# Graph attention on one core: the value products of two heads placed behind the slot's job products instead of ahead of them

## The chip, the cores and the metric

The kernel runs on one core of one Trainium2 chip. The metric is the device time of the program in microseconds (us), the median of several runs. The engines meant by the short names in the rows are TensorE (PE, its weight loads PEld), VectorE (DVE), ScalarE (ACT), GpSimd (POOL) and SyncE (SP, which here only issues DMAs). Each engine works through its own instructions in order, and the engines meet only through semaphores.

## The reference

For each of B = 32 graphs with N = 256 nodes of D = 512 features, a layer norm with ReLU is followed by attention with 16 heads of 32 features, whose scores get twice the adjacency matrix added, and by an output projection and a residual:

```python
h = jnp.maximum(_layernorm(x, axis=-1), 0.0)
q = split_heads(h @ Wq.T); k = split_heads(h @ Wk.T); v = split_heads(h @ Wv.T)
a = jnp.einsum('bhnd,bhmd->bhnm', q, k) * scale + (adj + adj)[:, None]
row_nonzero = jnp.any(a != 0, axis=-1, keepdims=True)
p = softmax(where(row_nonzero, a, -inf)); p = jnp.where(jnp.isnan(p), 0.0, p)
o = jnp.einsum('bhnm,bhmd->bhnd', p, v)
out = x + merge_heads(o) @ Wo.T
```

## The kernel before, in words

One batch is one graph. A batch is cut into 16 slots, one for each head hh (L537 to L551 on TensorE, L733 on ScalarE, L967 on VectorE, L1158 on GpSimd). All engines walk through the same slots, each in its own written order; nothing is planned at run time.

**TensorE in slot hh** does, in this order:

- T: four transposes of the head's softmax numerators into the PSUM tile `pT_ps` (`transpose_probs`, L455). They wait for the exponentials of head hh and for VectorE's reading of the tile two heads back.
- S: two score products for head hh + 3 into one of three banks `s_ps` (`scores`, L439).
- V, in even slots only: the value products of heads hh-2 and hh-1, 16 short matmuls into `o_ps` (`values`, L469). They wait for the low parts of both heads' transposed probabilities (`pT_split`).
- J: the slot's share of the large products, the "jobs" of the table `JOBS` (L25): projections q and k of the next batch or of the same one (`qk`), value projections (`v`), transposes of the attention output of a batch (`o`) and the output projection (`y`). A job with 24 or 12 products is cut over slots.

The jobs use two PSUM banks in turn. At a job's first product `begin` (L360) waits until the job that used the bank before has been read out (`taken`). Three such handovers matter here:

- slot 2: the last ten products of job v2, then the first three of v3, whose bank qk3 filled until slot 1; it is free after VectorE's two operations L862 and L864.
- slot 4: y0 of the batch before; its bank was filled by v3 until late in slot 3 and is free after VectorE's L870. Slot 3 is nine products of v3 and then the four transposes of o1, whose bank v2 filled until slot 2.
- slot 14: v0 of the next batch; its bank was filled by y1 until slot 13 and is free after ScalarE's L662. Slot 15 holds v1, whose bank is not one of these.

**ScalarE in slot hh**: if hh is odd, first `copy_outputs` (L664), which copies `o_ps` out to `o_raw` and so waits for the semaphore `pv_done` of V in slot hh-1; then the exponentials of head hh+1 (L681, two instructions); then the first half of taking every job that ended in slot hh-1 (`take`, L633: L646/L648 for qk, L655 for v, L659 for o, L662 for y); then `high_probs` (L686, L692), which rounds the transposed probabilities of head hh and waits for T. The order is

```python
if hh % 2:                      # L735 to L740
    copy_outputs(b, hh // 2 - 1, first and hh < 10)
exponentials(b, hh + 1, ...)    # L745
take(kind, n, b + d, ...)       # L751
high_probs(b, hh, ...)          # L757
```

In slot 4 the taking of v3 stands ahead of the exponentials (L743), in slot 10 `split_tokens` (L702) stands at the end, and in slot 13 `copy_adj` (L710) waits for the shift of head 15.

**VectorE in slot hh**: the shifted scores of head hh+2 and their row bounds (`shift`, L901), once in four slots `any_nonzero` (L922, L932), then the second half of taking jobs, then `low_probs` (L910), which waits for `high_probs` and makes `pT_split`; in slots 3, 6, 11 and 0 statistics (L782) or `low_tokens` (L880) of a later batch follow.

**GpSimd** folds the shifted scores, divides the outputs and adds the residual. **SyncE** issues all DMAs.

Of the kernel before, what the change touches and what calls it, by code (L numbers as in the profile page):

```python
# [60 lines left out]
def jobs_at(hh, first, last):  # L61

    return [j for j in JOBS[hh] if not (first and j[2] < 0) and not (last and j[2] > 0)]
# [11 lines left out]
def attention_block(nc, x, adj, wq, wk, wv, wo_t, out):  # L75
# [23 lines left out]
    with ExitStack() as ctx:  # L99
# [256 lines left out]
        def _(pe):  # L356
# [82 lines left out]
            def scores(b, hh, early=False):  # L439
                if isinstance(b, int) and b == 0 and G <= hh < HH:  # L440

                    pe.wait_ge(late_stacked[hh % G], STACKED)
                elif hh % HH < G:

                    pe.wait_ge(stacked[hh % G], stack_count(hh // HH, b))
                if not early:

                    pe.wait_ge(shifted, head_no(b, hh) + (1 - bank_before(hh)))
                stack = qk_stack[:, hh // HH, hh % G, :, hh % HH // G, :]
                for t in range(NT):  # L450
                    end = nc.tensor.matmul(s_ps[SCORE_BANK[hh]][:, t * N:(t + 1) * N], stack[:, 0, t * P:(t + 1) * P],  # L451
                                           stack[:, 1, :], start=True, stop=True)
                end.then_inc(scores_ready, 1)

            def transpose_probs(b, hh, early):  # L455

                pe.wait_ge(exp_done, head_no(b, hh) + 1)
                if not early:
                    pe.wait_ge(pT_split, head_no(b, hh) - 1)
                elif hh == 1:  # L460

                    pe.wait_ge(taken["v"], count("v", 0, 0))
                for m in range(NT):
                    for t in range(NT):
                        end = nc.tensor.transpose(pT_ps[hh % 2][:, m * N + t * P:m * N + (t + 1) * P],  # L465
                                                  probs[hh % 2][:, t, m * P:(m + 1) * P], ident[:, :])
                end.then_inc(pT_ready, 1)

            def values(b, hh, early):  # L469

                if hh % HH == 0:

                    pe.wait_ge(taken["v"], count("v", 2 * (hh // HH) + 1, b))
                if hh % 2 == 0 and not early:

                    pe.wait_ge(o_copied, b * PAIRS + hh // 2)

                pe.wait_ge(pT_split, head_no(b, hh) + 1)
                for t in range(NT):
                    q = (hh % 2) * NT + t  # L480
                    ps = o_ps[:, q * P:(q + 1) * P]
                    for m in range(NT):
                        hi = pT_hi[hh % 4][:, m, t * P:(t + 1) * P]
                        lo = pT_lo[hh % 4][:, m, t * P:(t + 1) * P]
                        v = v_parts[:, m, hh, :]
                        nc.tensor.matmul(ps[:, 0:LOW + HD], hi, v[:, 0:LOW + HD], start=m == 0, stop=False)  # L486
                        end = nc.tensor.matmul(ps[:, 0:HD + 1], lo, v[:, 0:HD + 1], start=False, stop=m == NT - 1)  # L487
                end.then_inc(pv_done, 1)
# [48 lines left out]
            def body(b, odd, first, last):  # L537
                for hh in range(HEADS):
                    transpose_probs(b, hh, first and hh < 2)
                    if hh + AHEAD < HEADS:  # L540
                        scores(b, hh + AHEAD)
                    elif not last:
                        scores(b + 1, hh + AHEAD - HEADS)

                    for was in range(hh - 2, hh) if hh % 2 == 0 else ():
                        if was >= 0:
                            values(b, was, first and was < 2)
                        elif not first:
                            values(b - 1, HEADS + was, False)
                    for kind, n, d, start, stop in jobs_at(hh, first, last):  # L550
                        job(kind, n, d, start, stop, b, odd)  # L551
                for i, (kind, n, d) in last_in.items():
                    last_in[i] = (kind, n, d - 1)

            for b in range(B):
                body(b, b % 2, b == 0, b == B - 1)
# [652 lines left out]
```

## Time and profile before

| what | value |
|---|---|
| median of 3 runs | 1252.07 us (1252.06 to 1252.55) |
| the profiled execution, its own time | 1249.15 us |
| its span, first to last instruction | 1247.4 us |
| mean granted TensorE clock | 0.997 of full speed |
| TensorE busy with matmuls | 1209.6 us (97%), 12856 of them |
| VectorE busy | 1088.7 us (87%) |
| ScalarE busy | 1029.7 us (83%) |
| GpSimd busy | 905.8 us (73%) |

The busy time of an engine is the sum of its instruction records without their overlaps. A record of TensorE is longer than the step to the next one, since matmuls overlap; what an instruction costs there is read from start to start. Records of ScalarE and VectorE too overlap the next one slightly. One batch takes 37.91 us in the middle of the run (slot 0 begins at 601.41 us, that of the next batch at 639.32).

### The profile page before, as it was taken

What the parts mean: (1) busy time and instruction counts of PE and PEld (TensorE: products, weight loads), DVE (VectorE), ACT (ScalarE), POOL (GpSimd) and SP (SyncE); (2) the same over time, 40 slices, a digit from 0 to 9 for tenths busy, and PEclk for the clock granted to TensorE, in tenths of its full rate; (3) what the DMA queues carried; (4) which work ended last, traced back from release to release, by engine and by line L of the source; (5) the groups of instructions that cost most, each with busy time, mean ns of one, the idle gap of its engine ahead of it and who ended that gap; (6) DMA issues with size and microseconds to landing.
All of it is one profiled execution on the core that took longest, in us unless ns stands there. A gap on an engine that the chain in (4) does not pass through costs nothing.

```text
span 1247.4 us, 42107 instructions
## 1 busy us (share of the span) xinstructions
PE 1209.6 (97%) x12856; PEld 1087.1 (87%) x12856; DVE 1088.7 (87%) x3500; ACT 1029.7 (83%) x2398; POOL 905.8 (73%) x1268
## 2 busy tenths in 40 slices
PE   6899999999999999999999999999999999999997
PEld 5788988888889888889888888888898888898896
DVE  7798888888888888888888888898888888888887
ACT  5788888888888888888888888888888888888886
POOL 5587777777777777777677777777777777776775
PEclk9899999999999999999999999999999999999999
DMA  6567555676656676565775565765556755556643
GB/s 227 122 143 166 140 129 142 141 174 150 146 120 146 151 169 149 134 139 138 161 169 135 121 154 135 177 154 135 127 148 149 170 144 135 137 137 169 146 106 90
DMA packets 157431, 181.73 MB, mean 146 GB/s; under 512 B 80641, under 2 KB 90369, under 8 KB 157313
## 3 DMA queue, kind: packets, MB, share of 16 engines
q1 hardware_dynamic: 157312, 179.90, 59.6%
q8 instruction: 105, 1.72, 0.6%
q14 instruction: 14, 0.11, 0.0%
HBM read 46.14 MB, written 16.78 MB: 50 GB/s over the span
## 4 chain that ended last, share of the span: by engine, by line
issue 49%; POOL 45%; POOLq 2%; DVE 2%; PE 1%; DMA 1%; ACT 0%; SPq 0%; DVEq 0%
POOL fold L1117 14%; POOL o_raw L1091 6%; POOL bounds L1123 6%; POOL y L1109 6%; POOL mask L1084 3%; POOL o L1097 3%; POOL h L1076 2%; POOL factor L1088 2%; POOL rstd L1065 2%; PE job_ps L374 1%; DMA x_in<-x 1%; POOL minus_mean L1060 1%; POOL var_eps L1062 0%; POOL wo_lo L1130 0%; POOLq L1119 0%
## 5 line engine op out<-in xcount | busy, mean ns | idle before, releaser
L1117 POOL TENSOR_TENSOR fold<-minus 128x512 f32<-128x512 f32 x256 | 327.2, 1278 | 247.5 <-DVE bounds L901 247.5
L681 ACT ACTIVATE probs<-minus,bounds 128x256 f32<-128x256 f32 x1024 | 464.6, 508 | 28.3 <-DVE bounds L901 28.2
L910 DVE TENSOR_TENSOR pT_lo<-pT_ps,pT_hi 128x512 f16<-128x512 f32 x512 | 350.0, 684 | 90.0 <-ACT pT_hi L692 85.9
L901 DVE CUSTOM_DVE_ANT_0 minus<-s_ps,adj_now 128x256 f32<-128x256 f32 x1024 | 389.3, 418 | 6.3 <-ACT probs L681 4.6
L692 ACT ACTIVATE pT_hi<-pT_ps 128x512 f16<-128x512 f32 x512 | 306.2, 598 | 86.1 <-PE pT_ps L465 84.4
L374 PE MATMUL job_ps<-hT,w_hi 128*128 128x256 f16 x2048 | 350.5, 273 | 0.4 <-DVE hT L857 0.4
L465 PE MATMUL pT_ps<-ident,probs 128*128 128x128 f32 x2048 | 308.0, 273 | 1.8 <-ACT probs L681 1.6
L374 PE MATMUL job_ps<-hT,w_lo 128*128 128x256 f16 x1024 | 279.1, 273 | 0.0
L465 PEld LDWEIGHTS pT_ps<-ident,probs 128*128 128x128 f32 x2048 | 242.0, 141 | 19.2 <-ACT probs L681 2.5
L451 PE MATMUL s_ps<-qk_stack 96*128 96x256 f32 x1024 | 247.5, 323 | 5.1 <-DMA qk_stack<-qk_parts 5.1
L1123 POOL TENSOR_TENSOR bounds<-fold 128x256 f32<-128x256 f32 x256 | 197.6, 772 | 25.1 <-POOL fold L1117 9.6
L374 PEld LDWEIGHTS job_ps<-hT,w_hi 128*128 128x128 f16 x2048 | 180.9, 98 | 24.5 <-issue 0.6
L374 PE MATMUL job_ps<-w_hi,hT 128*128 128x256 f16 x1016 | 190.1, 273 | 4.8 <-ACT y L662 4.6
L486 PE MATMUL o_ps<-v_parts,pT_hi 128*128 128x65 f16 x2048 | 156.9, 192 | 3.7 <-DVE pT_lo L910 0.9
L451 PEld LDWEIGHTS s_ps<-qk_stack 96*128 96x128 f32 x1024 | 155.0, 191 | 6.2 <-DMA qk_stack<-qk_parts 5.9
L487 PE MATMUL o_ps<-v_parts,pT_lo 128*128 128x33 f16 x2048 | 150.1, 179 | 0.0
L486 PEld LDWEIGHTS o_ps<-v_parts,pT_hi 128*128 128x128 f16 x2048 | 123.7, 97 | 18.6 <-DVE pT_lo L910 7.1
L374 PE MATMUL job_ps<-w_lo,hT 128*128 128x256 f16 x508 | 138.4, 272 | 0.0
L487 PEld LDWEIGHTS o_ps<-v_parts,pT_lo 128*128 128x128 f16 x2048 | 126.8, 96 | 0.0
L374 PEld LDWEIGHTS job_ps<-w_hi,hT 128*128 128x128 f16 x1016 | 96.9, 98 | 21.1 <-ACT y L662 7.6
L374 PE MATMUL job_ps<-wo_hi,oT_hi 128*128 128x512 f32 x256 | 107.4, 419 | 6.8 <-DVE v_parts L870 6.6
L374 PEld LDWEIGHTS job_ps<-hT,w_lo 128*128 128x128 f16 x1024 | 99.9, 98 | 11.8
(92 smaller groups left out, 1835.3 us busy)
## 6 DMA issues: line engine op xcount, KB each, us to landing
qk_stack<-qk_parts SPq DMA_DIRECT2D x756, 128.0 KB, 2.3
x_in<-x SPq DMA_DIRECT2D x32, 512.0 KB, 4.8
x_res<-x SPq DMA_DIRECT2D x32, 512.0 KB, 3.9
out<-y SPq DMA_DIRECT2D x64, 256.0 KB, 2.1
adj_in<-adj SPq DMA_DIRECT2D x32, 256.0 KB, 3.5
qk_stack<-qk_parts SPq DMA_DIRECT2D x24, 64.0 KB, 2.0
w_in<-wq SPq DMA_DIRECT2D x2, 512.0 KB, 5.6
w_in<-wk SPq DMA_DIRECT2D x2, 512.0 KB, 6.4
```

What stands on the lines that cost most here:

```text
L374: end = nc.tensor.matmul(dst, lhs[a](k), rhs[c](k), start=i == 0, stop=i == len(terms) - 1)
L451: end = nc.tensor.matmul(s_ps[SCORE_BANK[hh]][:, t * N:(t + 1) * N], stack[:, 0, t * P:(t + 1) * P], stack[:, 1, :], start=True, stop=True)
L465: end = nc.tensor.transpose(pT_ps[hh % 2][:, m * N + t * P:m * N + (t + 1) * P], probs[hh % 2][:, t, m * P:(m + 1) * P], ident[:, :])
L486: nc.tensor.matmul(ps[:, 0:LOW + HD], hi, v[:, 0:LOW + HD], start=m == 0, stop=False)
L487: end = nc.tensor.matmul(ps[:, 0:HD + 1], lo, v[:, 0:HD + 1], start=False, stop=m == NT - 1)
L681: end = nc.scalar.activation(probs[hh % 2][:, t, :], minus[hh // 2 % 2][:, hh % 2, t, :], ACT.Exp, bias=bounds[:, hh // 2 % 4, 2 * (hh % 2 ...
L692: nc.scalar.activation(pT_hi[hh % 4][:, :, :], pT_ps[hh % 2][:, :].rearrange("p (m n) -> p m n", m=NT), ACT.Copy).then_inc(pT_high, 1)
L901: end = nc.vector.tensor_tensor_reduce(out=minus[pair % 2][:, hh % 2, t, :], in0=s_ps[SCORE_BANK[hh]][:, t * N:(t + 1) * N], in1=adj_now[: ...
L910: nc.vector.tensor_tensor(pT_lo[hh % 4][:, :, :], pT_ps[hh % 2][:, :].rearrange("p (m n) -> p m n", m=NT), pT_hi[hh % 4][:, :, :], ALU.sub ...
L1091: nc.gpsimd.tensor_tensor(raw[:, :, :, 0:HD], raw[:, :, :, 0:HD], raw[:, :, :, LOW:LOW + HD], ALU.add).then_inc(o_added, 1)
L1117: nc.gpsimd.tensor_tensor(f1[:, :, :], src[:, :, 0:N // 2], src[:, :, N // 2:N], ALU.add).then_inc(folded1, 1)
L1123: nc.gpsimd.tensor_tensor(f2, f1[:, :, 0:N // 4], f1[:, :, N // 4:N // 2], ALU.add).then_inc(folded2, 1)
```

## The change

In the loop of TensorE over the slots, the value products of the last two heads are written behind the loop over the slot's jobs. No instruction is added or removed, no wait is changed, and no other engine's code is touched. Odd slots have no value products and stay as they are.

```diff
                     elif not last:
                         scores(b + 1, hh + AHEAD - HEADS)
 
+                    for kind, n, d, start, stop in jobs_at(hh, first, last):
+                        job(kind, n, d, start, stop, b, odd)
                     for was in range(hh - 2, hh) if hh % 2 == 0 else ():
                         if was >= 0:
                             values(b, was, first and was < 2)
                         elif not first:
                             values(b - 1, HEADS + was, False)
-                    for kind, n, d, start, stop in jobs_at(hh, first, last):
-                        job(kind, n, d, start, stop, b, odd)
                 for i, (kind, n, d) in last_in.items():
                     last_in[i] = (kind, n, d - 1)
```

## Rows read from the trace of the kernel before

**Rows 1.** The page, part 1: busy us, share of the span, instructions.
```profile
PE 1209.6 (97%) x12856; PEld 1087.1 (87%) x12856; DVE 1088.7 (87%) x3500; ACT 1029.7 (83%) x2398; POOL 905.8 (73%) x1268
```

**Rows 2.** Waits of PE over the whole span: us in total, times, longest us.
```profile
PE job_ps L374 <- DVE v_parts L870: 6.6, 29, 0.2
...
PE job_ps L374 <- ACT y L662: 4.6, 28, 0.2
...
PE o_ps L486 <- DVE pT_lo L910: 0.9, 2, 0.5
```

**Rows 3.** Timeline of PE, slots 2 to 5: start us, length us, operation, count, idle before.
```profile
607.21 0.38 PE L374 MATMUL job_ps<-w_hi,hT 128*128 128x256 f16 x2
...
608.63 0.60 PE L465 MATMUL pT_ps<-ident,probs 128*128 128x128 f32 x4
...
611.42 0.20 PE L486 MATMUL o_ps<-v_parts,pT_hi 128*128 128x65 f16 x1
...
611.85 0.18 PE L487 MATMUL o_ps<-v_parts,pT_lo 128*128 128x33 f16 x1
612.26 0.50 PE L374 MATMUL job_ps<-wo_hi,oT_hi 128*128 128x512 f32 x1 [0.23 <-DVE v_parts L870]
...
613.75 0.60 PE L465 MATMUL pT_ps<-ident,probs 128*128 128x128 f32 x4
```

**Rows 4.** Timeline of ACT, slots 3 and 4.
```profile
607.48 0.39 ACT L670 ACTIVATE o_raw<-o_ps 128x260 f32<-128x260 f32 x1
607.76 0.90 ACT L681 ACTIVATE probs<-minus,bounds 128x256 f32<-128x256 f32 x2
608.56 0.37 ACT L655 ACTIVATE v_parts<-job_ps 128x256 f16<-128x256 f32 x1
609.27 0.60 ACT L692 ACTIVATE pT_hi<-pT_ps 128x512 f16<-128x512 f32 x1 [0.33 <-PE pT_ps L465]
```

**Rows 5.** Timeline of DVE, slots 2 to 4.
```profile
607.24 0.42 DVE L864 SCALAR_TENSOR_TENSOR qk_parts<-job_ps,qk_parts 128x256 fp32r<-128x256 f32 x1
...
609.90 0.69 DVE L910 TENSOR_TENSOR pT_lo<-pT_ps,pT_hi 128x512 f16<-128x512 f32 x1 [0.50 <-ACT pT_hi L692]
...
611.78 0.42 DVE L870 SCALAR_TENSOR_TENSOR v_parts<-job_ps,v_parts 128x256 f16<-128x256 f32 x1
```

**Rows 6.** Timeline of ACT, slots 11 to 15.
```profile
626.99 0.40 ACT L670 ACTIVATE o_raw<-o_ps 128x260 f32<-128x260 f32 x1
...
628.05 0.61 ACT L692 ACTIVATE pT_hi<-pT_ps 128x512 f16<-128x512 f32 x1
...
635.35 0.58 ACT L662 ACTIVATE y<-job_ps 128x512 f32<-128x512 f32 x1
...
637.85 0.40 ACT L655 ACTIVATE v_parts<-job_ps 128x256 f16<-128x256 f32 x1
638.11 0.62 ACT L692 ACTIVATE pT_hi<-pT_ps 128x512 f16<-128x512 f32 x1
```

**Rows 7.** Timeline of PE, slots 11 to 15.
```profile
627.17 0.60 PE L465 MATMUL pT_ps<-ident,probs 128*128 128x128 f32 x4
...
634.64 0.48 PE L451 MATMUL s_ps<-qk_stack 96*128 96x256 f32 x2
635.99 0.28 PE L374 MATMUL job_ps<-w_hi,hT 128*128 128x256 f16 x1 [0.17 <-ACT y L662]
...
637.31 0.60 PE L465 MATMUL pT_ps<-ident,probs 128*128 128x128 f32 x4
```

**Rows 8.** One stretch of DVE, slot 15 to slot 2: stretch, its length, DVE busy, clock.
```profile
600.87:606.84 5.97, 5.66 (x20) 1.00 1.00 227
```

**Rows 9.** Timeline of weight loads and of PE, last batch, slot 14, which has no job.
```profile
1235.48 0.42 PEld L465 LDWEIGHTS pT_ps<-ident,probs 128*128 128x128 f32 x4
...
1235.51 0.64 PE L465 MATMUL pT_ps<-ident,probs 128*128 128x128 f32 x4
```

**Rows 10.** Stretches of the whole core after a 4.89 us wait: length, PE, PEld, DVE, ACT, POOL, clock.
```profile
46.00:50.00 4.00, 3.42 (x27) 2.82 (x28) 3.99 (x14) 3.13 (x8) 2.61 (x5) 0.50 0.96 216
...
600.00:637.90 37.90, 37.42 (x403) 33.72 (x401) 33.51 (x109) 31.78 (x76) 27.97 (x40) 1.00 0.64 147
```

## The prediction

> **What bounds the kernel now.** I read the page first: TensorE is busy for 97% of the span, VectorE for 87%, ScalarE for 83% [rows 1]. One batch in the middle confirms it: 37.42 of 37.90 us at full clock [rows 10]. So TensorE's own stream sets the time, and only what makes it longer or leaves a hole in it counts. The second view is the list of its waits. Two of them come back about once a batch, short ones: y0 in slot 4 waits for VectorE's L870 (29 times, 6.6 us), v0 in slot 14 for ScalarE's L662 (28 times, 4.6 us). A wait for the value products' own input exists twice, 0.9 us in all [rows 2]. This tells two things: the order of before has almost nothing left to win for the value products, and in slots 4 and 14 the job already starts at the very moment its bank comes free. The third view is the timeline of three engines over one batch, from which I take the steps below. I write T, S, V, J for the parts of a slot, as in the section on the kernel.
>
> **What moves.** Per even slot V (16 matmuls) costs 0.46 us from first start to the next possible one (611.42 to 611.85 plus one step of 0.03) [rows 3]. J now begins 0.46 us earlier behind S, and V ends a whole J later, at the moment the next T begins. Nothing is added, and no DMA is moved on any queue. SyncE's stacking and storing wait for the takings of jobs, which come at most some 0.8 us later by the steps below, and none of TensorE's recurring waits is for a DMA [rows 2]; I cost that at nothing.
>
> **Step 1, cover lost.** In slot 4, y0 starts at 612.26 because VectorE's L870 ends at 611.78 + 0.42 = 612.20 [rows 3, 5]. V stood ahead of it and filled 0.46 us of that wait. Now TensorE stands idle until the same moment and does V afterwards: +0.46 us. The same in slot 14: v0 starts at 635.99 because L662 ends at 635.35 + 0.58 = 635.93 [rows 6, 7]; +0.46 us. This holds even if no release moves at all.
>
> **Step 2, ScalarE held in odd slots.** ScalarE's first work in an odd slot is to copy V's result, and behind it in its queue stand the exponentials, a taking, and `high_probs`, for which VectorE waits. In slot 3 the copy started 0.27 us after V's end (607.21 to 607.48), the exponentials 0.28 later, the taking of v2 at +1.08 [rows 3, 4], and `high_probs` can follow the taking 0.26 behind (637.85 to 638.11) [rows 6]. Before, all this ran under J, and `high_probs` began 0.64 us behind T's start (608.63 to 609.27), held by T itself [rows 3, 4]. Now V ends when T3 begins, so `high_probs` starts at T3 + 0.27 + 1.08 + 0.26 = T3 + 1.61: 0.97 us later. An odd slot without a taking gets T + 1.35, which is some 0.5 to 0.7 later. The exponentials for the following T end by T + 1.5, and the shortest odd slot lasts 2.0, so T itself does not wait.
>
> **Step 3, slot 4 with both.** VectorE's order is `low_probs` of head 3, statistics, a shift, then L870. Before, `low_probs` started 0.63 behind `high_probs` (609.27 to 609.90), having waited 0.50 for it, and y0 started 2.36 later (612.26) [rows 3 to 5]. So y0 now starts at T3 + 1.61 + 0.63 + 2.36 = T3 + 4.60. It runs 1.49 us (612.26 to 613.75), V follows with 0.46, and T5 comes at T3 + 6.55. Before it was 613.75 - 608.63 = 5.12. Cost 1.43 us, step 1's part of it included. A new wait of the transposes o1 in slot 3 for v2's late taking (about 0.6 us) lies inside the same hole and costs nothing more.
>
> **Step 4, slot 14.** The copy in slot 11 goes from 626.99 to T11 + 0.27 = 627.44, so `high_probs` moves from 628.05 by 0.45 [rows 6, 7]. From there a chain without slack runs through VectorE (low parts, low tokens, shifts of heads 14 and 15), ScalarE's `copy_adj`, `high_probs`, exponentials and L662. Release 0.47 later and 0.46 of lost cover: 0.93 us. T15 - S14 grows from 637.31 - 634.64 = 2.67 to 3.6 us [rows 7].
>
> **Step 5, slot 2.** v3's first product follows ten of v2, 0.109 us each (13 from 607.21 to 608.63). Its bank was released at 607.24 + 0.42 + 0.06 = 607.72, and TensorE came at 608.30: slack 0.58 [rows 3, 5]. Now TensorE comes 0.46 earlier, 607.84. In slot 15 `high_probs` starts at T + 1.61 instead of T + 0.80 (637.31 to 638.11) [rows 6, 7], 0.81 later, and VectorE from there to the qk3 taking has 5.97 - 5.66 = 0.31 us idle [rows 8], so at least 0.50 and by my steps 0.65 arrive. New wait: 607.72 + 0.65 - 607.84, about 0.5 us. Bounds 0 and 0.7.
>
> **Step 6, the seams.** V behind J and T behind V are new neighbours. J's slot in the last batch is empty, and there T follows V directly: its load starts 0.03 us ahead of the first transpose, and the block is 0.64 long against 0.60 [rows 9, 3]. I take 0.03 us a seam, 8 in a batch: 0.24; the ends are 0 and 0.14 (one of T's loads, 0.42 us for overlapping four there, laid bare). Here the Trainium skill speaks against the change: "TensorE: Matmul & The Clock Gate", The mechanism, says weight loads overlap running matmuls only in other row groups. By that rule each T behind V would show its load. Rows 9 disagree, the load running beside V.
>
> **Sum.** 1.43 + 0.93 + 0.5 + 0.24 = 3.1 us in each of the 29 batches that carry everything, 90 us. Batch 0 (no y), batch 30 (no statistics) and batch 31 (no next batch) give some 0.7, 1.9 and 1.4: 4 us. Against the profiled execution: 1249.15 + 94 = 1343 us. That execution is 2.9 us under the median of the runs, so the median could as well be 1346; I stay with 1343.
>
> **Rivals.** *Only the cover is lost* (chance 0.10). ScalarE's delay is soaked up before it reaches a bank; what remains is step 1 and the seams: 29 x (0.92 + 0.24) less or more the edges, 1249 + 28 to 36 = 1277 to 1285. For it: ScalarE has 17% idle [rows 1]. Against: the chain in step 3 starts with a VectorE that was already waiting for ScalarE.
> *The clock falls* (0.05). After the one wait of 4.89 us, TensorE ran at a granted 0.50, its lower level of 1.2 GHz [rows 10]. The new hole in slot 4 is about 1.2 us, before y0. If it sufficed, and the work of a stretch as long as that row's (4 us at 0.50) took twice its time, that is another 2 us a batch: 1343 + 58 = 1401 us. "TensorE: Matmul & The Clock Gate" of the Trainium skill, A second HAM failure mode: psum-queue depth-cycling, tells of short idles between matmul groups that did this; no row here shows a fall after a hole this short.
> *The loads are laid bare* (0.02), the skill's rule of step 6: 8 x 0.14 in place of 0.24, 1249 + 94 + 29 x 0.9 = 1369 us.
> *Faster* (0.02). V waits for its input less (0.9 us) [rows 2], and the jobs of even slots end 0.46 us earlier, so their takings could too. If the releases in slots 4 and 14 came earlier by more than 0.46 us, the present waits of 6.6 + 4.6 us would shrink: at best 1249 - 12 = 1237. Against: v3 ends in an odd slot, and its release hangs on ScalarE's queue, which the change delays.
> *Nothing happens* (0.02): the holes swallow each other, 1249 to 1252.
>
> **Numbers.** The forecast has 0.79. Its own ends: low 1.4 us a batch (cover, and slot 4's delay halved), 1249 + 41 = 1290; high 3.8 (seams at 0.14, slot 2 at 0.7), 1249 + 112 = 1361. The range reaches down a little to take in the upper edge of the first rival: 1285 to 1361. A difference under 0.2% (2.5 us) can't be told from none. Slower 0.96, same 0.02, faster 0.02.
>
> **What the profile after would show.** Right: PE's wait for L870 some 1.1 to 1.2 us in place of 0.23, for L662 about 1.0, a new wait in about 30 batches for L864, and one in slot 3 for L870; ACT's wait for PE in front of L670 in nearly every odd slot; L692 in odd slots 1.35 or 1.61 behind T. A batch of 41.0 us. Wrong: a batch of 39.0 (steps 3 to 5 fall), a granted clock under 1 in the slices (step of the clock), or waits of T for L681, which I have excluded.

## The result, and the profile after

The changed kernel takes 1327.82 us (median of 4 runs, 1327.67 to 1329.08) against 1252.31 before (4 runs): a ratio of 1.0605, 95% interval 1.0586 to 1.0623, or 75.5 us more. The profiled execution took 1327.91 us with a span of 1326.1, which is 78.7 over that of before; 1.2 of these lie ahead of the first slot, in the start that the change does not touch.

Page of the changed kernel, part 1 and the clock of part 2; it answers to [rows 1]:
```profile
PE 1225.4 (92%) x12856; PEld 1076.8 (81%) x12856; DVE 1085.9 (82%) x3500; ACT 996.8 (75%) x2398; POOL 905.8 (68%) x1268
...
PEclk9899999999999999999999999999999999999999
```
Every engine does the same work in a longer span, and the row of the granted clock is the same, digit for digit, in the page of before. So the time went into waiting. The waits of PE, total, times, longest, against [rows 2]:
```profile
PE job_ps L374 <- ACT y L662: 31.4, 30, 1.1
PE job_ps L374 <- DVE v_parts L870: 30.8, 31, 1.0
PE job_ps L421 <- DVE v_parts L870: 11.0, 31, 0.4
```
Slot 14's and slot 4's waits grew from 0.16 and 0.23 us each to about 1.0, and the transposes of o1 at the end of slot 3 have a new one. The list of waits over all engines shows the other half:
```profile
ACT o_raw L670 <- PE o_ps L487: 280.8, 218, 2.6
```
It is the second largest of the whole run; before, it read
```profile
ACT o_raw L670 <- PE o_ps L487: 0.9, 2, 0.6
```
ScalarE now stands in front of its copy in nearly every odd slot.

The timeline of PE, slots 2 to 5, answers to [rows 3]:
```profile
605.49 0.63 PE L374 MATMUL job_ps<-w_hi,hT 128*128 128x256 f16 x2
...
606.62 0.64 PE L465 MATMUL pT_ps<-ident,probs 128*128 128x128 f32 x4
...
608.85 0.66 PE L421 MATMUL job_ps<-ident,o 128*128 128x128 f32 x4 [0.36 <-DVE v_parts L870]
...
611.22 0.50 PE L374 MATMUL job_ps<-wo_hi,oT_hi 128*128 128x512 f32 x1 [1.02 <-DVE v_parts L870]
...
612.71 0.20 PE L486 MATMUL o_ps<-v_parts,pT_hi 128*128 128x65 f16 x1
...
613.17 0.63 PE L465 MATMUL pT_ps<-ident,probs 128*128 128x128 f32 x4
```
ScalarE's, slot 3, answers to [rows 4]:
```profile
606.89 0.39 ACT L670 ACTIVATE o_raw<-o_ps 128x260 f32<-128x260 f32 x1 [1.48 <-PE o_ps L487]
607.17 0.90 ACT L681 ACTIVATE probs<-minus,bounds 128x256 f32<-128x256 f32 x2
607.97 0.37 ACT L655 ACTIVATE v_parts<-job_ps 128x256 f16<-128x256 f32 x1
608.23 0.59 ACT L692 ACTIVATE pT_hi<-pT_ps 128x512 f16<-128x512 f32 x1
```
VectorE's, slots 2 to 4, answers to [rows 5]:
```profile
605.37 0.41 DVE L864 SCALAR_TENSOR_TENSOR qk_parts<-job_ps,qk_parts 128x256 fp32r<-128x256 f32 x1
...
608.86 0.69 DVE L910 TENSOR_TENSOR pT_lo<-pT_ps,pT_hi 128x512 f16<-128x512 f32 x1
...
610.74 0.42 DVE L870 SCALAR_TENSOR_TENSOR v_parts<-job_ps,v_parts 128x256 f16<-128x256 f32 x1
```
Read them as one chain: V ends as T3 starts (606.62); copy at T3 + 0.27, L692 at T3 + 1.61 (it was T3 + 0.64), L910 at T3 + 2.24, L870 done at 611.16, y0 at T3 + 4.60, T5 at T3 + 6.55. The last two numbers are those of step 3.

The first PE row holds slot 2's wait. It is the last product of v2 and the first of v3; such a pair lasts 0.38 us in [rows 3], here 0.63. L864 ends at 605.78, and v3 starts about 0.06 later. The list of waits counts idle time only from the end of the record before, and has L864 in front of v3 just once, with 0.7 us: these 0.25 us lie mostly beside the record of the product before. So the "new wait in about 30 batches" of the forecast is there (slot 2 takes 2.80 us on the mean of batches 2 to 29, where it took 2.56), but only the timeline shows it.

Slots 14 and 15, PE, against [rows 7]:
```profile
634.12 0.49 PE L451 MATMUL s_ps<-qk_stack 96*128 96x256 f32 x2
635.68 0.28 PE L374 MATMUL job_ps<-w_hi,hT 128*128 128x256 f16 x1 [1.07 <-ACT y L662]
...
637.44 0.63 PE L465 MATMUL pT_ps<-ident,probs 128*128 128x128 f32 x4
```
T15 - S14 is 3.32 us; it was 2.67, and the forecast said 3.6.

The table below is the measure for all that follows. It is worked out from the starts of T (L465) in one middle batch of each kernel: the length of a slot is the distance to the next slot's T. Slots not named differ from before by at most 0.09 us, most in slot 12. The means over batches 2 to 29 agree with this one batch within 0.04 us. "Ahead" and "behind" say where V stands against J.

| kernel | median us | batch | slot 2 | slot 3 | slot 4 | slot 14 |
|---|---|---|---|---|---|---|
| before | 1252.3 | 37.91 | 2.55 | 2.11 | 3.03 | 3.05 |
| the change | 1327.8 | 40.37 | 2.80 | 2.73 | 3.82 | 3.67 |
| e1 ahead in 4, 14 | 1292.7 | 39.14 | 2.80 | 2.73 | 3.37 | 3.00 |
| e2 behind in 4, 14 | 1287.3 | 39.10 | 2.56 | 2.11 | 3.47 | 3.71 |
| e3 behind in 2 | 1283.1 | 38.88 | 2.56 | 2.73 | 3.37 | 3.06 |
| e4 change, copies late | 1299.2 | 39.44 | 2.80 | 2.15 | 3.47 | 3.68 |
| e5 before, copies late | 1251.6 | 37.92 | 2.56 | 2.12 | 3.00 | 3.06 |
| e6 before, early takes | 1233.9 | 37.21 | 2.55 | 2.11 | 2.61 | 2.76 |
| e7 change, early takes | 1290.5 | 39.13 | 2.80 | 2.73 | 3.25 | 3.01 |
| e8 change, both | 1261.3 | 38.16 | 2.80 | 2.15 | 2.87 | 2.99 |
| f1 behind in 14 | 1265.5 | 38.36 | 2.55 | 2.12 | 3.00 | 3.47 |
| f2 change, ahead in 0, 14 | 1306.3 | 39.60 | 2.56 | 2.73 | 3.83 | 3.21 |
| f3 change, L880 moved | 1306.1 | 39.63 | 2.80 | 2.73 | 3.82 | 2.95 |
| f4 before, stats and L880 moved | 1222.2 | 36.90 | 2.56 | 2.10 | 2.61 | 2.44 |

The change adds 2.46 us to this batch: 0.25 in slot 2, 1.41 to 1.43 in slots 3 and 4 (before repeats within 0.02), 0.62 to 0.64 in slot 14, and 0.14 to 0.18 in all other slots together. Twenty-eight batches (2 to 29) grew by some 2.49 each, which is 70 us, the four others and the end by 7.8.

### The profile page after: what moved, and what is told of

The parts are those of the page before. It is cut to its first block, busy times and chain, and to the rows that moved or that the text cites. A ratio compares the mean times of both kernels' runs of the same rounds, so it can differ in the third digit from the quotient of the medians.

```text
span 1326.1 us, 42107 instructions
## 1 busy us (share of the span) xinstructions
PE 1225.4 (92%) x12856; PEld 1076.8 (81%) x12856; DVE 1085.9 (82%) x3500; ACT 996.8 (75%) x2398; POOL 905.8 (68%) x1268
## 4 chain that ended last, share of the span: by engine, by line
issue 52%; POOL 42%; POOLq 2%; PE 1%; DVE 1%; DMA 1%; ACT 0%; SPq 0%; DVEq 0%
POOL fold L1117 14%; POOL o_raw L1091 6%; POOL y L1109 5%; POOL bounds L1123 5%; POOL mask L1084 2%; POOL o L1097 2%; POOL h L1076 2%; POOL factor L1088 2%; POOL rstd L1065 2%; PE job_ps L374 1%; DMA x_in<-x 1%; POOL minus_mean L1060 1%; POOL var_eps L1062 0%; POOLq L1116 0%; POOLq L1082 0%
## 5 line engine op out<-in xcount | busy, mean ns | idle before, releaser
L910 DVE TENSOR_TENSOR pT_lo<-pT_ps,pT_hi 128x512 f16<-128x512 f32 x512 | 349.6, 683 | 119.4 <-ACT pT_hi L692 115.6
L465 PE MATMUL pT_ps<-ident,probs 128*128 128x128 f32 x2048 | 316.5, 277 | 1.8 <-ACT probs L681 1.7
L670 ACT ACTIVATE o_raw<-o_ps 128x260 f32<-128x260 f32 x255 | 98.9, 388 | 282.0 <-PE o_ps L487 280.8
L692 ACT ACTIVATE pT_hi<-pT_ps 128x512 f16<-128x512 f32 x512 | 304.5, 595 | 0.1
L465 PEld LDWEIGHTS pT_ps<-ident,probs 128*128 128x128 f32 x2048 | 227.9, 140 | 8.6 <-ACT probs L681 2.3
L374 PE MATMUL job_ps<-w_hi,hT 128*128 128x256 f16 x1016 | 195.9, 274 | 34.0 <-ACT y L662 31.4
L1123 POOL TENSOR_TENSOR bounds<-fold 128x256 f32<-128x256 f32 x256 | 197.6, 772 | 25.1 <-POOL fold L1117 9.6
L486 PE MATMUL o_ps<-v_parts,pT_hi 128*128 128x65 f16 x2048 | 149.8, 191 | 0.7 <-DVE pT_lo L910 0.5
L486 PEld LDWEIGHTS o_ps<-v_parts,pT_hi 128*128 128x128 f16 x2048 | 131.9, 96 | 20.6 <-issue 17.1
L487 PE MATMUL o_ps<-v_parts,pT_lo 128*128 128x33 f16 x2048 | 145.9, 178 | 0.0
L374 PE MATMUL job_ps<-wo_hi,oT_hi 128*128 128x512 f32 x256 | 104.5, 408 | 31.0 <-DVE v_parts L870 30.8
```

Source lines behind the costliest of these rows:

```text
L374: end = nc.tensor.matmul(dst, lhs[a](k), rhs[c](k), start=i == 0, stop=i == len(terms) - 1)
L670: nc.scalar.activation(o_raw[pair // 2 % 2][:, pair % 2, :, :], o_ps[:, :].rearrange("p (q c) -> p q c", c=P)[:, :, 0:LOW + HD], ACT.Copy) ...
L692: nc.scalar.activation(pT_hi[hh % 4][:, :, :], pT_ps[hh % 2][:, :].rearrange("p (m n) -> p m n", m=NT), ACT.Copy).then_inc(pT_high, 1)
L910: nc.vector.tensor_tensor(pT_lo[hh % 4][:, :, :], pT_ps[hh % 2][:, :].rearrange("p (m n) -> p m n", m=NT), pT_hi[hh % 4][:, :, :], ALU.sub ...
L1123: nc.gpsimd.tensor_tensor(f2, f1[:, :, 0:N // 4], f1[:, :, N // 4:N // 2], ALU.add).then_inc(folded2, 1)
```

## The experiments

The theory that goes in: the change costs by the cover it takes from two late banks, and by ScalarE, held in odd slots ahead of work for which VectorE waits. The rival: the lost cover alone.

**Where V stands, slot by slot (e1, e2, e3).**
```diff
-for was in range(hh - 2, hh) if hh % 2 == 0 else ():          # ahead of the jobs
+for was in range(hh - 2, hh) if hh % 2 == 0 and hh not in BEHIND else ():
...
 for kind, n, d, start, stop in jobs_at(hh, first, last):
     job(kind, n, d, start, stop, b, odd)
+for was in range(hh - 2, hh) if hh in BEHIND else ():         # behind them
```
with BEHIND = (0, 2, 6, 8, 10, 12), then (4, 14), then (2,). The bodies of the two loops over `was`, left out here, are those of before; the remarks behind # are mine.

> V stands behind J in slots 0, 2, 6, 8, 10 and 12, and ahead of it, as before, in slots 4 and 14, where the banks come free late. If the change costs by two parts (V no longer fills the hole ahead of y0 and v0; ScalarE is held in odd slots and so frees y0's bank 0.97 us later), the second part stays in slots 3 and 4: 0.97 there, some 0.2 in slot 14, 0.05 to 0.1 of seams, 29 x 1.2 = 35 us over before: about 1287. PE's wait for L870 then reads about 1.2 us with V ahead of it. If only the lost cover counts, the cover is back and the time is that of before, 1252 to 1256.

> The counterpart: V stands behind J in slots 4 and 14 only. Both theories expect the lost cover, 0.46 us twice in each of 29 batches, 27 us: about 1279. By the theory with two parts nothing more comes: the copy in slot 15 is late and VectorE's L864 in slot 2 with it by 0.4 us, but TensorE comes to slot 2's bank as late as before, with 0.58 us of slack. If the holding of ScalarE were all of the cost, this would give at most 1260. If every wait came from slots 4 and 14 alone, it would give the 1328 of the change.

> V stands behind J in slot 2 only. No cover is lost at a hole, and slot 2's own slack of 0.12 us is enough as long as L864 is not late. If holding ScalarE in slot 3 is real, high_probs of head 3 starts 0.97 us later, L870 in slot 4 too, and y0 with it: 29 x 0.97 = 28 us, about 1280, with PE's wait for L870 at about 1.2 us behind V. If only the lost cover counts: 1252.

Measured: e1 1292.73 us, ratio 1.0318 (1.0300 to 1.0335); e2 1287.31, 1.0275 (1.0258 to 1.0293); e3 1283.05, 1.0241 (1.0224 to 1.0258). The rival that only the cover is lost falls with e1 and e3: with V ahead of y0 and v0, or moved in one slot where no bank is late, 40 and 30 us are still lost. e3 is the cleanest: one V moved in slot 2, and the loss appears two slots later. Its rows on ScalarE, slot 3, and PE, slot 4 (lines of this kernel are 5 higher; T3 starts at 586.17):
```profile
586.44 0.39 ACT L675 ACTIVATE o_raw<-o_ps 128x260 f32<-128x260 f32 x1 [1.52 <-POOL o L1102]
586.72 0.90 ACT L686 ACTIVATE probs<-minus,bounds 128x256 f32<-128x256 f32 x2
587.52 0.37 ACT L660 ACTIVATE v_parts<-job_ps 128x256 f16<-128x256 f32 x1
587.78 0.59 ACT L697 ACTIVATE pT_hi<-pT_ps 128x512 f16<-128x512 f32 x1
```
```profile
590.77 0.50 PE L374 MATMUL job_ps<-wo_hi,oT_hi 128*128 128x512 f32 x1 [0.59 <-DVE v_parts L875]
```
`high_probs` is at T3 + 1.61 again, y0 at T3 + 4.60. (The profile names GpSimd's L1102 as what the copy waited for; the copy has two waits, and it started 0.27 behind V's end as always.) Slots 3 and 4 together are 6.10 against 5.14: 0.96, where 0.97 was expected. The list has the wait for L875 at 0.6 and not at the 1.2 that was expected in e1 and e3, because 0.62 of the hole already lies in slot 3 (2.73 against 2.11), ahead of the transposes of o1. In e2 slot 4 lost 0.44, the cover.

Two things did not come as expected. In e1 slot 2 still waits (2.80). And in e2 slot 14 takes 3.71, 0.66 more, where the cover alone is 0.44 to 0.46.

**Taking the hold away (e4, e5).**
```diff
-                    if hh % 2:
+                    if hh % 2 and not (hh % 4 == 3):
...
                     high_probs(b, hh, first and hh < 4)
+                    if hh % 4 == 3:
+                        copy_outputs(b, hh // 2 - 1, first and hh < 10)
```
e4 is this edit on the change, e5 on the kernel before.

> The change whole, but in slots 3, 7, 11 and 15 ScalarE copies the value sums behind high_probs in place of ahead of the exponentials, so nothing is held there. By the theory with two parts only the lost cover and the seams stay: 29 x (0.92 + 0.1) = 30 us over before, about 1282, slot 2's wait near 0. L692 in slot 3 starts 0.64 behind T again, y0 at T3 + 3.6. If ScalarE's queue had nothing to do with it, the time stays at 1328.

> Control for the late copies: the kernel before with ScalarE's copies behind high_probs in slots 3, 7, 11 and 15. With V ahead of J the copy found V ready, so moving it frees nothing: 1250 to 1254. If the late copies shorten the kernel by themselves, by something like 10 us or more, the run with the change and late copies says less about the holding.

Measured: e4 1299.23 us, 1.0371 (1.0353 to 1.0388) of before; e5 1251.64, 0.9990 (0.9980 to 0.9999), 1.5 us less, with an interval that stops just short of no change at all. e5 makes e4 readable: late copies by themselves give next to nothing. With the change they take 29 us off, nearly all of it in slots 3 and 4 (5.62 against 6.55), where only the cover is left. y0 starts at T3 + 3.67. This settles the hold for slot 4. The 17 us by which e4 missed 1282 sit mostly in two places of the table: slot 2 (2.80) and slot 14 (3.68), both untouched by copies that are late in slots 3, 7, 11 and 15. So neither of the two needs the holding there. That speaks against step 4, which had it in slot 11, and against slot 15 as the only source in step 5.

**Freeing the two banks earlier (e6, e7, e8).** e6 on the kernel before, e7 on the change, e8 on the change with e4's edit. Left out of the cut below: the place where y1 was taken so far now skips it.
```diff
+                    if hh == 14 and not first:
+                        take("y", 1, b - 1)             # ScalarE, ahead of the exponentials
...
-                        if hh == 3:
+                        if hh == 5:
                             tokens_stats(b + 2, range(0, 1))
```

> The kernel before with both late banks freed earlier: ScalarE takes y1 ahead of the exponentials in slot 14 (release 635.19 in place of 635.99, TensorE could start v0 at 635.43), and VectorE does the statistics of slot 3 in slot 5 (release of y0's bank 0.60 us earlier than 612.26, TensorE could start at 611.91). Both waits should vanish: 0.56 + 0.35 us in 29 batches, 26 us: about 1226. If the next wait takes their place: 1235 to 1252.

> The change with the same two moves. The holes of slots 4 and 14 are there bank releases, 1.02 and 1.07 us of waiting; they come 0.60 and 0.80 us earlier and do not vanish: 29 x 1.4 = 41 us less than the change, about 1287. If the waits in these slots came from something other than VectorE's and ScalarE's order in slots 3 and 14, little or nothing: over 1315.

> The change with early takes and late copies: all three causes treated. Releases come 1.6 us (slot 4) and about 1.0 us (slot 14) earlier than under the change; what stays is some 0.25 us in each of the two slots and 0.1 of seams: 29 x 0.6 = 17 us over the kernel before with early takes, about 1243. If the order V behind J has a cost of its own that no bank explains, it is seen here: over 1255.

Measured: e6 1233.90 us, 0.9849 (0.9833 to 0.9865); e7 1290.48, 1.0297 (1.0279 to 1.0314); e8 1261.26, 1.0063 (1.0046 to 1.0080). e7's slots 4 and 14 fell by 0.57 and 0.66, so the holes are bank releases. e6 won 0.42 in slot 4 as it should, but only 0.29 in slot 14. Its waits of PE say why:
```profile
PE o_ps L486 <- DVE pT_lo L912: 4.8, 24, 0.5
```
The waits for the banks are gone from the list, and V of slot 14 now waits for its own input, the low parts of head 13: the whole row of work in slot 13 is late, not the taking alone. In the kernel before V waits there too, at its middle, where the second head begins:
```profile
635.17 0.18 PE L487 MATMUL o_ps<-v_parts,pT_lo 128*128 128x33 f16 x1
635.43 0.20 PE L486 MATMUL o_ps<-v_parts,pT_hi 128*128 128x65 f16 x1
```
The step is 0.26 where all others are some 0.03, and the list has nothing of it. From its first start to its last, V of slot 14 takes 0.69 us (the median over batches 2 to 29), and 0.43 in slots 2 and 4. So the prediction's reading of the list, that the order of before has almost nothing left to win for the value products, missed a wait of 0.26 us a batch, which stands right ahead of the one for y1's bank; 0.43 is what this V takes in f4 below.

e8 was expected at 1243 and missed by 18. Part of this is the 8 us by which e6 itself missed 1226. The rest is in the table: e8's batch is 0.95 longer than e6's, where 0.6 was expected. Slot 2 adds 0.25, which the expectation had left out; slots 4 and 14 add 0.26 and 0.23, the 0.25 each that was expected; slot 3 adds 0.04 and the seams the rest. e8 is over the 1255 that it had named as the sign of a cost that no bank explains, but slot 2's 0.25 is a wait for a bank too, so only the seams are left as such a cost.

**What makes slot 14 late (f1, f3, f4), and slot 2 (f2).** The timelines of GpSimd and VectorE in slot 11, first of the kernel before:
```profile
628.92 1.28 POOL L1117 TENSOR_TENSOR fold<-minus 128x512 f32<-128x512 f32 x1
```
```profile
629.30 1.44 DVE L880 SCALAR_TENSOR_TENSOR h_parts<-h,h_parts 128x512 f16<-128x512 f32 x1
```
of the changed kernel, with T11:
```profile
626.68 0.63 PE L465 MATMUL pT_ps<-ident,probs 128*128 128x128 f32 x4
```
```profile
628.61 1.28 POOL L1117 TENSOR_TENSOR fold<-minus 128x512 f32<-128x512 f32 x1
```
```profile
629.26 1.18 DVE L880 SCALAR_TENSOR_TENSOR h_parts<-h,h_parts 128x512 f16<-128x512 f32 x1
```
and of e2:
```profile
609.75 1.28 POOL L1122 TENSOR_TENSOR fold<-minus 128x512 f32<-128x512 f32 x1
```
```profile
609.89 1.69 DVE L885 SCALAR_TENSOR_TENSOR h_parts<-h,h_parts 128x512 f16<-128x512 f32 x1
```
L880 lasts 1.44, 1.18 and 1.69 us, but its end is 0.54, 0.55 and 0.55 behind the end of GpSimd's fold each time (630.20 to 630.74, 629.89 to 630.44, 611.03 to 611.58). It is the fold that sets when VectorE goes on, not the moment at which L880 could begin. The same 0.55 to 0.56 us stand in every batch from 4 to 27 of all twelve kernels that have L880 in slot 11, with records from 0.90 to 1.74 us; in each the fold had started first. The Trainium skill, "SBUF — State Buffer", Who interferes with whom, says that a VectorE instruction with two SBUF inputs contends with a GpSimd instruction that reads SBUF, and it calls the shared pair of ports "an exclusive lock". L880 has two such inputs (`h` and `h_parts`), and these rows agree: what is left behind the fold does not depend on how long L880 has stood beside it.

GpSimd in turn works almost without a pause from its fold in slot 7 to the one in slot 11 (from 619.72 to 628.92 before), and that first fold starts when VectorE's shift of head 9 is done: 5.97 us behind T5 before, 6.23 under the change (both at a T5 of 613.75 and 613.17):
```profile
619.40 1.28 POOL L1117 TENSOR_TENSOR fold<-minus 128x512 f32<-128x512 f32 x1 [1.08 <-DVE bounds L901]
```
The shift is late by 0.26, which I put down to ScalarE being held in slot 5, by the V of slot 4. That gave the expectations of the last four runs; moved is

```diff
-                        if hh == 11:
+                        if hh == 13:
                             low_tokens(b + 2, 0)
```
for f3 (on the change) and f4 (on the kernel before, with e6's statistics in slot 5, but ScalarE's order as it was). f1 and f2 are the edit of e1 with BEHIND = (14,) and (2, 4, 6, 8, 10, 12).

> V stands behind J in slot 14 only. With V behind J in slots 4 and 14, slot 14 took 3.71 us against 3.05, of which 0.46 is lost cover and 0.2 a later taking of y1. My account of the 0.2: the copy held in slot 5 makes VectorE's shift of head 9 late, with it GpSimd's fold in slot 7, GpSimd then works without a pause to its fold in slot 11, VectorE's L880 beside that fold ends only 0.55 us behind it, and from there the chain to y1's taking has no slack. So without V behind J in slot 4 the 0.2 is gone: slot 14 takes 3.49, slot 4 3.03, 29 x 0.45 = 13 us over before, 1266. If the 0.2 belongs to slot 14 itself, it takes 3.7: 1272.

> The change, but V ahead of J in slots 0 and 14. With V ahead in 4 and 14 slot 2 still waited 0.25 us, which step 5 of the prediction had put down to slot 15. If the copy held in slot 1 is enough for that wait, it goes only now: slot 2 takes 2.56 in place of 2.80, slot 14 3.25 in place of 3.67, slots 3 and 4 stay at 6.55: 29 x 0.66 = 19 us less than the change, 1309. If slot 2 waits for reasons of its own (V behind J there): 2.80 stays, 1316.

> The change with one VectorE instruction, L880 of slot 11, done at the end of slot 13, off the chain to y1's taking. If that chain (GpSimd's fold, L880, shifts, copy_adj, L692, L681, L662) makes slot 14's hole, y1 is taken some 1.0 us earlier or more, TensorE's wait for L662 is nearly gone, and slot 14 takes 2.5 to 2.7 in place of 3.67: 29 x 1.1 = 32 us less than the change, 1296. If ScalarE's own order (exponentials ahead of L662) makes the hole, little: 1315 or more.

> The kernel before with L880 of slot 11 at the end of slot 13 and the statistics of slot 3 in slot 5, both on VectorE. Slot 4 takes 2.61 as with the early takes, and slot 14, where y1 is then taken before TensorE needs its bank, 2.47 in place of 3.05: 29 x (0.42 + 0.58) = 29 us under before, 1224. If moving L880 holds something else (the shift of the next batch's head 0, o0's taking, v0's), 1235 or more.

Measured: f1 1265.54 us, 1.0104 (1.0087 to 1.0121), slot 14 at 3.47: with V of slot 4 back ahead, slot 14 is 0.24 shorter than in e2, and L880 ends 0.26 earlier behind T11 (3.57 against 3.83). The cause of the lateness stands ten slots ahead of its effect. That V of slot 4 is the cause is shown by this pair of runs; the way through GpSimd is read from the rows. f2 1306.30, 1.0429 (1.0412 to 1.0446): slot 2 is 2.56 again with V still behind J in it, so its wait comes from the hold in slot 1, by V of slot 0. Slot 15's hold was gone in e1 too and slot 2 waited there, so slot 1's is enough for it. No run has V behind J in slot 2 with slot 15's hold alone. But e2 and f1 have slot 15's hold without slot 1's, and V ahead of J in slot 2, so that TensorE comes too late to wait. There L864 starts 1.59 and 1.58 behind T2, against 1.16 in before and in f2, where neither hold is. Its row in e2, where T2 starts at 586.17:
```profile
587.76 0.41 DVE L869 SCALAR_TENSOR_TENSOR qk_parts<-job_ps,qk_parts 128x256 fp32r<-128x256 f32 x1
```
Under the change, with both holds, it is 1.55. So either hold makes L864 late by some 0.4, and the two do not add up. f3 1306.14, 1.0431 (1.0413 to 1.0448): slot 14 falls from 3.67 to 2.95, 0.72 where 1.0 to 1.2 was expected, and the time is 10 us over the 1296 expected. L880 stood in the chain that made most of the hole. (Moving it takes away its own 0.68 us along with its wait for the fold, so f3 does not say how much of the 0.72 was that wait.) What is left of the wait is 9.8 us in 30 times:
```profile
PE job_ps L374 <- ACT y L662: 9.8, 30, 0.3
```
ScalarE in f3, slots 13 and 14:
```profile
621.61 0.39 ACT L670 ACTIVATE o_raw<-o_ps 128x260 f32<-128x260 f32 x1 [0.89 <-PE o_ps L487]
...
624.50 0.58 ACT L662 ACTIVATE y<-job_ps 128x512 f32<-128x512 f32 x1
```
From the copy, held by V of slot 12, to L662 it works without a pause. I read the rest as that hold, but no run separates it.

f4 1222.21 us, 0.9757 (0.9740 to 0.9773): 1224 was expected. It beats both kernels, the one before by 2.4%. Its page and its waits of PE:
```profile
PE 1196.5 (98%) x12856; PEld 1082.8 (89%) x12856; DVE 1071.0 (88%) x3500; ACT 1032.1 (85%) x2398; POOL 909.9 (75%) x1268
```
```profile
PE pT_ps L507 <- ACT w_in L600: 9.4, 1, 9.4
PE s_ps L451 <- DMA qk_stack<-qk_parts: 5.9, 1, 5.9
PE pT_ps L465 <- ACT probs L681: 1.6, 3, 0.6
PE o_ps L486 <- DVE pT_lo L910: 0.9, 2, 0.5
```
No wait is left that comes back in every batch; the two large ones are at the start.

## Why the prediction was right, and which terms were off

The forecast of 1343 us was 15 too high; the way held, and of the mechanism the lost cover and the hold ahead of slot 4. Slot 14's second half came by another way than forecast. A little of the closeness is luck of the base: the 94 us were put on a profiled execution 2.9 us under the median. On the median they would have given 1346, against 75.5 us more that came. Point by point:

- **What bounds the kernel now:** mostly right. V of slot 14 did wait for its input in nearly every batch, 0.26 us at its second head, which the list of waits did not show.
- **Step 1, cover lost:** right. Slot 4 of e2 lost 0.44, slot 14 of f1 0.42 to 0.44, for 0.46.
- **Steps 2 and 3, slots 3 and 4:** right to the hundredth: L692 at T3 + 1.61, y0 at T3 + 4.60, T5 at T3 + 6.55. (In slots 5, 7 and 9, for which T + 1.35 was forecast, L692 came at T + 1.27.) The wait of o1 is there (31 times) and, as put, costs nothing more, since y0 waits behind it. e3 and e4 show the part of the hold, 0.96 us, by making and by removing it.
- **Step 4, slot 14:** 0.93 forecast, 0.64 measured, and the reason given for the second half was wrong. The step that failed is "From there a chain without slack runs through VectorE". ScalarE's late L692 in slot 11 (0.47 later behind T11) reached VectorE as forecast: L880 starts 2.58 behind T11, against 2.13 before. But it ends 3.76 behind, against 3.57: it had been waiting for GpSimd's fold anyway, and soaked up most of the delay. In e1, with the same late L692 and V of slot 4 ahead, slot 14 is not longer than before (3.00). The 0.2 that did arrive came from V of slot 4, as f1 shows against e2, and by the rows through GpSimd. I had seen L880's length in the timeline and taken it as work; half of it was a wait.
- **Step 5, slot 2:** 0.5 forecast, 0.25 measured. The late release is real, but slot 15's hold, to which it was put down, is not alone: f2 and e1 show slot 1's to be enough, and L864 in e2 and f1 shows the same of slot 15's. Of the 0.65 us by which I had L864 late, 0.39 arrived: L864 now starts 1.55 behind T2 (603.82 to 605.37), against 1.16 before (606.08 to 607.24).
- **Step 6, the seams:** 0.24 forecast, 0.14 to 0.18 measured, which is some 0.23 to 0.26 for the seams and 0.09 given back in slot 12. T behind V is 0.03 to 0.04 longer (613.17 to S at 613.56, 0.39, against 0.35 behind J). What pays back is slot 12: y1 starts right behind S there, and its first step is 0.24 us (629.39 to 629.63), where behind V it had been 0.32 (630.31 to 630.63). That no load is laid bare agrees with rows 9 and not with the rule weighed in step 6.

The three sizes together are 29 x (0.29 + 0.25 + 0.1) = 19 us too many. In full, between the two profiled executions: batches 1 to 29 grew by 72 us where 90 were forecast, batches 0, 30 and 31 with the end by 5.7 where 4 were, and 1.2 us came ahead of the first slot, where none were. The rival "only the cover is lost" fell with e1, e3 and e4, "the clock falls" with the unchanged clock row, although holes of 1.0 us stand in every batch, and "faster" with the direction.

## What to carry to other kernels

An instruction moved later on the busiest engine is free there only if nothing queues behind its result: here ScalarE's copy of that result stood first in ScalarE's queue, and each of its slots was held until the moved work was done. Moving work also takes it out from under a wait that it had been filling; look where the engine arrives exactly at a release before moving anything from ahead of it. And a small wait in the list can stand for a larger hole, since the list counts from the end of overlapping records: the 0.23 and 0.17 us of slots 4 and 14 before turned into 0.42 and 0.61 of shorter slots in f4, 2.4% in all, once two VectorE instructions were moved off the way to the late banks (in slot 14 they had held V's own input too).

## What the runs showed of the hardware that I had not expected

VectorE's L880 lasts 1.18, 1.44 or 1.69 us in three kernels, and ends 0.54 to 0.55 us behind GpSimd's fold in all three. The start of its record moves with VectorE's own work and the end with GpSimd's, and the profile counts all of it as busy and names no wait, so a long record next to a GpSimd instruction is partly waiting, and a delay ahead of it can vanish. In f4, where it stands in slot 13, it runs from 585.00 to 585.89 and ends 0.54 behind another GpSimd instruction, L1123 (584.61 to 585.35). In slot 0, with no GpSimd instruction beside it, the same instruction takes 0.68 us:
```profile
601.72 0.68 DVE L880 SCALAR_TENSOR_TENSOR h_parts<-h,h_parts 128x512 f16<-128x512 f32 x1
```
